# Moving eight blocks of VectorE work inside the attention windows of a gated attention and expert kernel

## The reference, cut to what matters

```python
x = x + tanh(g_xattn) * xattn(ctx_768, layernorm(x), mask, ...)      # x: 4 x 1024 x 256
x = x + tanh(g_ffn)   * ffn(layernorm(x), w_router, w1, b1, w2, b2)
# xattn: queries from layernorm(x); keys and values from the 64 context rows and from layernorm(x);
#        4 heads of 64; q and k divided by their root mean square; softmax; out @ Wo.T + bo
# ffn:   8 experts (256 -> 1024 -> 256, gelu), each token weighted over its two best by the router
```

## Time and profile before

| | |
|---|---|
| median of 3 runs | 908.65 us (907.42 to 910.56) |
| profiled execution, its own time | 908.65 us |
| its span in the trace | 906.9 us |
| PE busy | 853.6 us, 94% |
| DVE busy | 647.4 us, 71% |
| ACT busy | 513.4 us, 57% |
| POOL busy | 330.3 us, 36% |
| granted PE clock over the span | 0.99 |

### The profile page before, as it was taken

One profiled execution on the slowest core, in us unless ns is written; L12 is line 12 of the kernel. 1 busy time (PEld: TensorE's weight loads), 2 busy tenths in 40 slices (PEclk: granted clock), 3 DMA queues, 4 the chain that ended last, 5 costly groups with the idle time before them and its releaser, 6 DMA issues.

```text
span 906.9 us, 19559 instructions
## 1 busy us (share of the span) xinstructions
PE 853.6 (94%) x5968; PEld 654.4 (72%) x5968; DVE 647.4 (71%) x1500; ACT 513.4 (57%) x1371; POOL 330.3 (36%) x241
## 2 busy tenths in 40 slices
PE   3898899999999999999999999999999999999995
PEld 3654455554455544555459999899999999999995
DVE  6766767668877668677798778866755775576695
ACT  2668776787757878568762754343533443343462
POOL 2332323332286322763144328532322323222233
PEclk9899999999999999999999999999999999999999
DMA  4801000130012201120034449352432535252272
GB/s 128 247 1 50 1 1 1 47 96 1 1 48 94 94 1 47 42 94 18 1 106 124 135 101 274 77 144 46 129 57 47 136 77 108 44 145 46 35 233 24
DMA packets 71895, 70.26 MB, mean 77 GB/s; under 512 B 18592, under 2 KB 66976, under 8 KB 71840
## 3 DMA queue, kind: packets, MB, share of 16 engines
q1 hardware_dynamic: 57696, 52.73, 19.7%
q0 software_dynamic: 13152, 16.86, 10.5%
q10 hardware_dynamic: 992, 0.00, 0.1%
HBM read 44.04 MB, written 26.31 MB: 78 GB/s over the span
## 4 chain that ended last, share of the span: by engine, by line
PE 53%; issue 14%; DVE 13%; POOL 9%; ACT 5%; DMA 5%; SPq 1%; DVEq 0%; POOLq 0%; ACTq 0%
PE psS L1694 17%; PE psF L1890 8%; PE psO L1890 8%; PE psO L1827 5%; POOL rr L680 5%; PE psS L1811 5%; PE psF L1694 4%; DVE p_sum L1140 3%; POOL routed L690 3%; DMA lnf<-routed 3%; PE psF L1858 1%; ACT sq L827 1%; ACT p_ring L871 1%; PE psO L1839 1%; DMA xr<-in_x 1%
## 5 line engine op out<-in xcount | busy, mean ns | idle before, releaser
L888 ACT ACTIVATE V<-psS,b_col 128x256 f32<-128x256 f32 x280 | 117.1, 471 | 209.4 <-PE psS L1694 192.5
L698 POOL DMA_INDIRECT out<-V,token_i x70 | 121.9, 1742 | 259.4 <-DVE V L1331 238.3
L680 POOL TENSOR_TENSOR rr<-ssm,minus_half 128x4 f32<-128x4 f32 (+1 forms) x72 | 117.2, 1628 | 249.6 <-DVE ssm L1104 249.6
L871 ACT ACTIVATE p_ring<-psS,shift 128x1024 f32<-128x1024 f32 x128 | 136.7, 1112 | 71.5 <-PE psS L1811 70.9
L1827 PE MATMUL psO<-p_ring,V 128*64 128x512 f32 x576 | 149.2, 615 | 0.0
L1140 DVE TENSOR_TENSOR p_sum<-p_sum,p_ring 128x1024 f32<-128x1024 f32 (+1 forms) x112 | 135.9, 1214 | 0.9
L1890 PE MATMUL psF<-ln_hi,K 128*128 128x256 f32 x560 | 123.4, 284 | 0.2 <-DVE K L1310 0.2
L1811 PEld LDWEIGHTS psS<-Q,K 64*128 64x128 f32 x864 | 77.2, 188 | 62.6 <-issue 43.5
L1811 PE MATMUL psS<-Q,K 64*128 64x512 f32 x864 | 122.0, 414 | 0.0
L1890 PE MATMUL psO<-ln_hi,K 128*128 128x256 f32 x560 | 120.3, 278 | 0.0
L1310 DVE TENSOR_TENSOR K<-V,K 128x512 fp32r<-128x512 f32 x140 | 97.2, 694 | 4.8
(11 more groups left out here) (289 smaller groups left out, 1760.3 us busy)
## 6 DMA issues: line engine op xcount, KB each, us to landing
xr<-in_L_ffn_w SPq DMA_DIRECT2D x11, 1024.0 KB, 4.8
xn<-in_L_ffn_w SPq DMA_DIRECT2D x11, 1024.0 KB, 5.8
lnf<-routed SPq DMA_DIRECT2D x35, 258.0 KB
routed<-pad_rows SPq DMA_DIRECT2D x17, 258.0 KB, 9.4
xr<-in_x SPq DMA_DIRECT2D x8, 512.0 KB, 4.4
xb<-in_x SPq DMA_DIRECT2D x4, 1024.0 KB, 6.0
out<-xb SPq DMA_DIRECT2D x4, 1024.0 KB, 4.7
b_raw<-in_L_ffn_b SPq DMA_DIRECT2D x11, 128.0 KB, 6.1
```

The source lines that it names most:

```text
L680: pool.tensor_tensor(rr[0:p, c % 2, n], ssm[0:p, c % 2, n], minus_half[0:p, n], ALU.pow).then_inc(rr_ready, 1)
L698: pool.indirect_dma_start(out_rows, bass.IndirectOffsetOnAxis(ap=token_i[:, m:m + 1], axis=0), y_out[:, m, :], None, bounds_check=NTOK - 1 ...
L871: act.activation(p_ring[0:p, u % RING, :], psS[u % 2][0:p].rearrange("p a n -> p (a n)"), ACT.Exp, bias=bias).then_inc(exp_done, 1)
L888: act.activation(g32[:, q % 2, (c % 2) * TM:(c % 2 + 1) * TM], psH[q][:, (c % 2) * TM:(c % 2 + 1) * TM], ACT.Gelu_apprx_tanh, bias=b1_col[ ...
```

## The change

It touches the DVE stream alone; no instruction is added or taken out, no semaphore and no size changes.

- `residual_base`: both halves now stand in group 5 of every even window, behind `second_offsets`. Before, they stood in groups 0 and 5 of the odd windows 1, 3, 5 (sequences 0, 1, 2), and in groups 5 and 8 of window 6 (sequence 3).
- `residual(b-1, 1)` in group 1 of windows 2, 4, 6 now stands behind `quotients(2w-1)`, before between `denominators` and `quotients`.
- `router_logits(b-1)` in group 3 of windows 3 and 5 now stands ahead of `heads_lo` and `mean_squares`, before behind them.
- `router_slots(b-1)` of windows 3 and 5 now opens group 7, before it stood in group 6 behind the second `add_probabilities`.
- The first half of the first expert's second weights is cut in group 5 of window 7, the second half right behind the last `add_probabilities`; before, they were cut ahead of `activate(0, 0)` and ahead of `activate(0, 2)`.

```diff
-                    if not even and past and last and i == 6:
+                    if not even and past and i == (6 if last else 7):
                         router_slots(b - 1)
                     if g >= 1:
                         add_probabilities(2 * g - 2)
-                    if not even and past and last and i == 2:
+                    if not even and past and i == (2 if last else 3):
                         router_logits(b - 1)
...
-                    if not even and past and not last and i == 3:
-                        router_logits(b - 1)
                     if g >= 1 and not ahead:
                         add_probabilities(2 * g - 1)
-                    if not even and past and not last and i == 6:
-                        router_slots(b - 1)
...
                         denominators(2 * w - 1)
-                    if even and past and i == 1:
-                        residual(b - 1, 1)
                     if w >= 1 and i == (1 if even else 2):
                         quotients(2 * w - 1)
...
-                        if i in (0, 2, 3):
+                        if i < 4:
                             residual(b - 1, i)
...
-                    if last and even and i in (5, 8):
-                        residual_base(b, i // 8)
-                    if more and not even and i in (0, 5):
-                        residual_base(b, i // 5)
+                    if even and i == 5:
+                        for half in range(2):
+                            residual_base(b, half)
...
+                    if w + 1 == WINDOWS and i == 5:
+                        cut(w2_parts[0:1], 0, w2_ready)
...
                 for u in (2 * NG - 2, 2 * NG - 1):
                     add_probabilities(u)
+                cut(w2_parts[1:2], 1, w2_ready)
                 dve.wait_ge(w_cut, 1)
-                cut(w2_parts[0:1], 0, w2_ready)
+
                 activate(0, 0)
                 activate(0, 1)
-                cut(w2_parts[1:2], 1, w2_ready)
                 activate(0, 2)
```

## The result

The changed kernel takes 917.11 us (median of 6 runs, 913.53 to 918.47), the kernel before 909.61 (6 runs, 907.42 to 912.62) on the same chip. The ratio is 1.0079, with a 95% interval of 1.0058 to 1.0099: slower, by 0.8%. Its profiled execution took 915.9 us with a span of 914.2, against 908.65 and 906.9; the granted clock is 0.99 in both. In the changed kernel the PE lines are numbered 5 less (L1694 is L1689, L1705 is L1700, L1743 is L1738, L1811 is L1806, L1827 is L1822).

The account below looks back on a forecast made before the run. PE was taken as the bound, waiting on `qkd` through the ring and on PSUM banks that DVE frees. Terms 3.4 + 2.1 + 1.5 - 0.3 + 0.3 = 7.0 on 908.65 gave 915.6 us, range 911.3 to 918.0.

Parts of the forecast that it names:

- Bases in the even windows: Group 5 of even windows: bases delay `ssm`, 1.15 in windows 2 and 4, 1.13 in window 6, nothing in 0; 3.4 us.
- Rival 1: The bases in group 5 of even windows are hidden by DVE's idle time: 912.2 us, chance 0.10.
- rival 4: The bases cost 2.26 in windows 2, 4 and 6, as no idle time helps: 919 us, chance 0.06.
- Residual behind `quotients`: Windows 2, 4, 6: bank 1 is read later, so the projection of group 2 starts 0.7 late each; 2.1 us.
- Logits: Group 3 of windows 3 and 5: logits ahead of `heads_lo` delay `K` and PE by 0.76 each; 1.5 us.
- Windows 3 and 5, groups 5 to 7: The missing base brings `qkd` earlier, but the later slots hold the bank for group 7's projection; together -0.3 us.
- rivals 2 and 3: 2: banks don't bind, no cost for residual and logits, 910.0, chance 0.08; 3: odd windows decide, 906.3, chance 0.04.
- Cuts: Window 7: the earlier cut delays `turned_lo(0)`, so PE starts `first_layer(0)` 0.3 us late.
- Row loads: Scatters and row loads shift with the slots by 1.1 us, taken as hidden behind two expert tiles.

## Why the prediction was right

The forecast was 915.6 us, 7.0 over the profiled execution; the changed kernel's profiled execution took 915.9, and the medians of the two kernels differ by 7.5. The mechanism was the one named: PE waits longer in the groups named, for the lines named. Step by step:

- **Bases in the even windows**: 3.4 reckoned, 3.39 measured, alone and in the whole. Without a base `ssm` comes 2.71 behind the add in windows 4 and 6 alike, with one or two 1.60: the slack of 1.11 covers one base and no more, in window 6 the one that stood there already. So each of the three windows pays for one. Rival 1 (both hidden) and rival 4 (neither) are out. The prediction set the distance of 1.13 between two bases against a rule of the Trainium skill, "VectorE: DVE Perf Modes", section "The DRAIN you can't avoid"; that section goes on to say that a next operation which is not held starts earlier, so the rows do not contradict it.
- **Residual behind `quotients`**: 2.1 reckoned, 2.31 measured. The term was 0.07 too small each time: the two instructions took 0.87 together there, not 0.79.
- **Logits**: 1.5 reckoned, 1.56 measured. The root grew to 1.91 us and stayed hidden.
- **Windows 3 and 5, groups 5 to 7**: -0.3 reckoned, -0.18 and -0.21 measured, so -0.39. The gain of 0.97 appears at the transposes. With the slots back in group 6 each window gains 1.11, so the late bank takes 0.9 of it back. This was the step on which rivals 2 and 3 hung: they had -2.4 here, and even with the slots in their old place it is -2.22. Both are out, since the residual, the logits and the slots, each moved alone, made PE wait for a bank's reader.
- **Cuts**: 0.3 reckoned, and the first expert tile did start 0.39 late, 0.33 of it idle time of PE. What failed here is that the delay was put into the sum as lasting, though the prediction itself says that the same DVE work is done behind it. At the second layer of the second tile 0.03 is left against the first profile of the kernel before (67.18 to 67.15) and 0.24 against its repeat (66.94), and in the windows nothing.
- **Row loads**: taken as hidden. The second to ninth expert tiles of the changed kernel's first profile start within 0.04 of the first profile of the kernel before, from the start of window 7; behind them executions differ by too much to tell.
- **The rest**: -0.11 in window 4, group 0, comes with the logits' move (it is there with the logits alone, and with no other part). I did not foresee it. DVE's first instruction behind `qkd` starts 0.43 behind the start of `qkd` in the kernel before and 0.35 behind it with the logits moved (257.79 to 258.14); everything on DVE up to `K` comes 0.1 earlier by it, and with it the bank:
```profile
256.60 0.42 DVE L1114 TENSOR_TENSOR qkd<-psF,rr 128x256 f32<-128x256 f32 x1 [0.94 <-POOL rr L680]
257.03 0.65 DVE L1052 BATCH_NORM_AGGREGATE mv<-stats 128x2 f32<-128x6 f32 x8
```
What lets that instruction start sooner stays open.

Together 3.39 + 2.31 + 1.56 - 0.39 - 0.11 = 6.76, of 6.79 measured in the windows, where the prediction's terms without the cuts make 6.7. That the whole came within half a microsecond of 7.0 is partly luck: the start was 0.87 shorter and the expert part 1.33 longer, and between two executions of one and the same kernel the start moved by up to 1.9 (the changed one) and the expert part by 3.4 and 4.5.

## What to carry to other kernels

Price a moved block by what stands behind it on its engine up to the next release that the bound engine needs (here the next `ssm` or the next reader of a bank), less the idle time in between; in this case PE never waited for the data that a moved block makes, and the idle time must be read in each window, as one with an extra piece of work in it can have none. A reader of a shared bank that comes one piece of work later can cost most of what a move brings (0.9 of 1.11 here). And before work is put into a wait, look at what the wait is for: if the filler slows that down, the wait is not free.

## What was unexpected of the hardware

- Adds of 2.35 us put into a wait of 2.02 us of DVE for POOL left a wait of 0.90 behind them, since POOL's root went from 1.00 to 2.15 us beside them, and they cost PE 1.15 to 1.20 three times.
- The windows repeat to 0.11 us in 328 between two executions of the kernel before, while the expert tiles behind them differ by 3.4, and by up to 4.5 between the changed kernel's two (1.33 and 5.8 over the first profile of before). A change of 0.3% in such a kernel shows in one pair of profiles by its stages, not by its time.
